# Products of messages and of the last channels on quarters of TensorE's array, in a graph network layer

## The chip, the core and the metric

The kernel runs on one core of a Trainium2 chip. The metric is the time of one execution on the device, in microseconds (us). Before the change it is 905.8 us, the median of three runs (902.68 to 907.19).

## What is computed

50,000 nodes with 160 channels (64 scalars and 32 vectors of three components), and 50,000 edges sorted by their target. For each edge a small network makes 192 weights of 16 features; the source node's channels are mixed, multiplied by these weights and by four numbers of the edge, and averaged over the edges of each target. A second mixing, a gate, and a product of the node's own channels follow, and a normalisation of each row.

```python
h = jax.nn.silu(edge_scalars @ (Wfc1 / jnp.sqrt(jnp.float32(FC_IN))))
w = h @ (Wfc2 / jnp.sqrt(jnp.float32(FC_H)))
...
f0 = x0 @ Wl1_0 * a * inv8
f1 = jnp.einsum('num,uv->nvm', x1, Wl1_1) * a[..., None] * inv32
e0 = f0[edge_src]
e1 = f1[edge_src]
...
mid0 = w0 * e0 * sh0
mid1 = w3 * jnp.einsum('eum,em->eu', e1, sh1) / jnp.sqrt(3.0)
mid2 = w1[:, :, None] * e0[:, :, None] * sh1[:, None, :]
mid3 = w2[:, :, None] * e1 * sh0[:, :, None]
...
alpha = scal @ Wa * a * inv96
out_s = scal @ Wl2_s * a * inv96
out_v = jnp.einsum('num,uv->nvm', vec, Wl2_v) * a[..., None] * inv96
conv = jnp.concatenate([out_s, out_v.reshape(n, 3 * MUL1)], axis=1)
return sc + alpha * conv
...
x = _layernorm(x + _L0_gnn_ref(x, node_vec1, ...), axis=-1)
```

Here `scal` and `vec` are the averages of mid0, mid1 and of mid2, mid3 over the edges of a node, and `sc` is the node's own channels times Wsc0 and Wsc1.

## The kernel before

The program has two stages, each written as steps that every engine runs through in its own order; semaphores alone tie the engines together.

**Edge stage.** A tile is 128 edges, a pair two tiles (t = 0, 1), a quad two pairs (k = 0, 1). A step d (98 quads, and three steps to run out) works on several quads at once:

- GpSimd gathers the source rows of quad d with four indirect DMAs (L620) into a ring of four quads.
- VectorE prepares quad d + 2 (`prepare`: sha, qprod, and its reduction; L996, L1005, L1011).
- TensorE makes the first layer (`first_layer`, L706) and the transposes of the gathered rows (`turn`, L712, L714) of quad d; ScalarE takes them out of PSUM (`take_turned`: L873, and L875 as te).
- TensorE makes, of quad d - 1, the products with source features (L732 on quarters of the array, L738 on halves) and the edge weights (L751, on halves) in `weigh`. ScalarE copies the former (L898, two copies of 512 columns).
- VectorE multiplies both into mid, for quad d - 2 (`multiply`, L1021).
- TensorE makes the products of messages of quad d - 3 (`combine`, L769 and L772): mid is the stationary operand, all 128 rows of it, and the weights wy are the moving one, 97 and 161 columns for each tile. ScalarE takes 65 of the columns into z (L883); VectorE makes the other 96 of z (L1039) and adds the message (L1045), 160 channels and a gate, in a row of 163 numbers with a count and a label that are set apart (L1029). SyncE stores the rows in DRAM.

All products are in float32, and each of these stands in the trace as two records; a transpose is one. The results of `combine` for k = 0 lie in the banks that hold the products with source features (2 and 3), those for k = 1 in banks 6 and 7; both kinds are a part of a wait:

```python
if k == 0:
    pe.wait_ge(e_out[t], min(q + 2, NS))
```

TensorE's order in a step is first layer, transposes and combine for k = 0, the same for k = 1, and `weigh`.

**Node stage.** A group is four tiles of 128 nodes (98 groups). SyncE loads windows of message rows; VectorE compares labels with columns; TensorE sums the messages of each node with the resulting 0/1 matrices (L831, 162 columns), transposes the scaled rows of the group (L817), and multiplies them with the self weights: the first 128 channels of the four tiles on quarters (L847), the last 32 channels of all four in one product over the full array (L849). ScalarE scales the sums (L943) and normalises (L921), VectorE adds the self products to x (L1391) and takes statistics (L1292), GpSimd scales the rows (L661, L664), adds (L686) and normalises a quarter (L675).

## Time and profile before

| | before |
|---|---|
| runs, us | 902.68, 905.8, 907.19 |
| profiled execution: time, span, us | 905.83, 903.9 |
| edge stage | to about 553 us of the span |
| node stage | from there to the end |
| granted clock of TensorE, mean | 0.992 |
| DMA, mean over the span | 207 GB/s |

The profile is of one execution. Its rows give, for an instruction or a group of them, the start and the time it took; an engine's instructions overlap at their ends, so the distance of two starts is often less than the first one's duration. In the chain, a piece is the time between what released an instruction and what it released.

### The profile page before, as it was taken

To read this page: it belongs to the slowest core of one execution; us is meant where nothing else is said; L and a number is where in the kernel's file an instruction comes from. 1 tells how busy PE (TensorE), PEld (TensorE's weight loads), DVE (VectorE), ACT (ScalarE), POOL (GpSimd) and SP (SyncE) were. 2 spreads that over 40 slices of the span, in tenths; PEclk is the share of its full clock that TensorE was granted. 3 is DMA by queue.
4 is the path that set the end of the run, shared out by engine and by line. 5 is a ranking of instruction groups with operands and counts; after the bars stand their busy time and mean duration, and the time that the engine had idled before them with its cause. 6 is when DMAs were issued, how large, how long until landed. Compare 5 with 4: busy or idle time off the path is not lost.

```text
span 903.9 us, 32652 instructions
## 1 busy us (share of the span) xinstructions
PE 855.1 (95%) x10688; PEld 726.4 (80%) x10688; DVE 810.6 (90%) x2797; ACT 630.4 (70%) x1961; POOL 715.3 (79%) x804
## 2 busy tenths in 40 slices
PE   2999999999998999999999988999999999999994
PEld 1788787788887877888888877888888888888884
DVE  3788999999996999999999987999999999999997
ACT  1555555555554655565565554999999999999997
POOL 6777777777776776777777712999999999999994
PEclk9999999999998999999999999999999999999998
DMA  6455544455456666567764413899999999999973
GB/s 183 121 166 165 167 137 130 133 131 143 131 135 129 187 204 190 164 172 203 208 181 132 134 64 120 249 308 314 315 318 326 310 315 312 321 304 318 319 258 146
DMA packets 87539, 186.77 MB, mean 207 GB/s; under 512 B 17646, under 2 KB 48138, under 8 KB 87371
## 3 DMA queue, kind: packets, MB, share of 16 engines
q1 hardware_dynamic: 50715, 93.00, 32.0%
q0 software_dynamic: 18944, 35.81, 18.1%
q10 hardware_dynamic: 17712, 55.87, 17.9%
q8 instruction: 87, 1.43, 0.7%
q14 instruction: 81, 0.66, 0.2%
HBM read 119.66 MB, written 64.95 MB: 204 GB/s over the span
## 4 chain that ended last, share of the span: by engine, by line
PE 70%; DVE 12%; issue 9%; POOL 5%; DMA 3%; ACT 1%; DVEq 0%; ACTq 0%; POOLq 0%
PE ps L831 20%; PE ps L772 7%; PE ps L847 7%; PE ps L751 6%; PE ps L817 6%; POOL gat L620 5%; PE ps L849 5%; PE ps L769 4%; PE ps L732 4%; PE ps L738 4%; DVE mid L1021 3%; DMA gat<-spread,srcs 3%; PE ps L714 3%; DVE z L1039 3%; PE ps L712 2%
## 5 line engine op out<-in xcount | busy, mean ns | idle before, releaser
L620 POOL DMA_INDIRECT gat<-turned,srcs x196 | 190.6, 973 | 68.9 <-issue 61.7
L620 POOL DMA_INDIRECT gat<-spread,srcs x196 | 189.5, 967 | 61.8 <-issue 59.1
L898 ACT ACTIVATE te<-ps 128x512 f32<-128x512 f32 x196 | 106.4, 594 | 124.8 <-PE ps L738 124.8
L831 PE MATMUL ps<-win,eas 60*128 60x162 f32 x2352 | 189.0, 306 | 0.7 <-DVE eas L1364 0.7
L772 PE MATMUL ps<-wy,mid 128*128 128x161 f32 x784 | 182.4, 314 | 0.0
L831 PEld LDWEIGHTS ps<-win,eas 60*128 60x128 f32 x2352 | 164.9, 186 | 17.0 <-issue 10.5
L686 POOL TENSOR_TENSOR gat<-eas,gat 128x640 f32<-128x640 f32 x98 | 152.4, 1555 | 15.2 <-ACT eas L943 12.3
L1045 DVE SCALAR_TENSOR_TENSOR msg<-ps,sha,z 128x161 f32<-128x161 f32 x392 | 151.0, 385 | 13.9
L769 PE MATMUL ps<-wy,mid 128*128 128x97 f32 x784 | 141.6, 262 | 0.2 <-DVE mid L1021 0.2
L1021 DVE TENSOR_TENSOR mid<-ps,te 128x512 f32<-128x512 f32 x196 | 133.1, 680 | 3.2 <-PE ps L751 3.2
L921 ACT ACTIVATE te<-gat,shift,rstd 128x160 f32<-128x160 f32 x292 | 131.2, 527 | 1.4 <-DVE shift L1311 1.3
L943 ACT ACTIVATE eas<-ps,coef 128x160 f32<-128x160 f32 x392 | 122.9, 402 | 9.4 <-DVE coef L1404 1.5
L769 PEld LDWEIGHTS ps<-wy,mid 128*128 128x128 f32 x784 | 123.5, 191 | 1.3 <-issue 0.7
L883 ACT ACTIVATE z<-ps 128x65 f32<-128x65 f32 x392 | 89.7, 229 | 46.1 <-PE ps L772 45.5
L772 PEld LDWEIGHTS ps<-wy,mid 128*128 128x128 f32 x784 | 119.2, 192 | 0.0
L873 ACT ACTIVATE h_sb<-ps 128x128 f32<-128x128 f32 x196 | 54.4, 278 | 75.4 <-PE ps L714 65.8
L1039 DVE TENSOR_TENSOR z<-ps,sha 128x96 f32<-128x96 f32 x392 | 97.7, 249 | 9.5 <-ACT z L883 2.8
L751 PE MATMUL ps<-h_sb,wt 64*128 64x256 f32 x784 | 102.8, 381 | 0.0
L875 ACT ACTIVATE te<-ps 128x384 f32<-128x384 f32 x196 | 94.9, 484 | 0.0
L1364 DVE TENSOR_TENSOR eas<-columns,ps 128x768 f32<-128x768 f32 x98 | 92.2, 941 | 0.1
L1292 DVE BATCH_NORM_STATS2 stats<-gat 128x6 f32<-128x320 f32 x196 | 87.1, 486 | 0.0
L664 POOL TENSOR_TENSOR eas<-xin 128x512 f32<-128x512 f32 x82 | 86.4, 1054 | 0.0
(108 smaller groups left out, 1515.1 us busy)
## 6 DMA issues: line engine op xcount, KB each, us to landing
win<-rows SPq DMA_DIRECT2D x392, 114.6 KB, 4.1
rows<-msg SPq DMA_DIRECT2D x98, 326.0 KB
out<-te ACTq DMA_DIRECT2D x47, 640.0 KB, 6.2
xin<-x_g ACTq DMA_DIRECT2D x76, 322.0 KB, 5.1
kept_x<-x_g SPq DMA_DIRECT2D x16, 322.0 KB
gat<-turned,srcs POOLq DMA_INDIRECT x196
gat<-spread,srcs POOLq DMA_INDIRECT x196
eas<-ea_t SPq DMA_DIRECT2D x7, 384.0 KB, 4.7
```

The source lines that it names most:

```text
L620: pool.indirect_dma_start(out=gat[:, slot, first:first + of.shape[1]], out_offset=None, in_=of, in_offset=bass.IndirectOffsetOnAxis(ap=src ...
L686: nc.gpsimd.tensor_tensor(res[:, slot], agg[:, b3], pre[:, b3], ALU.add).then_inc(res_ready, 1)
L751: last = nc.tensor.matmul(w_ps[:, t, 2 * c * P:2 * (c + 1) * P], wt[half, w:w + P], h_sb[half, b].rearrange("p k e -> p (k e)"), start=Tru ...
L769: nc.tensor.matmul(y[:, t, 0:W_Y1 - W_YA], mid[:, q % 2, t, 0, k, :], wy[:, 0:W_Y1 - W_YA], start=True, stop=True)
L772: nc.tensor.matmul(y[:, t, W_Y1 - W_YA:YW], mid[:, q % 2, t, 1, k, :], wy[:, of:of + VEC + 1 + MUL0], start=True, stop=True).then_inc(y_re ...
L831: last = nc.tensor.matmul(agg_ps[b1][:, 2 * h + k, 0:SW], hot[side(h), b1, k, c, :], win[side(h), (RING * i + b - 1) % WIN_RING, k, c, 0:S ...
L898: nc.scalar.activation(e_sb[:, t, :], e_ps[:, t], ACT.Copy).then_inc(e_out[t], 1)
L921: last = nc.scalar.activation(fin[:, past, k, :], res[:, past, k, :], ACT.Identity, bias=shift[:, past, k:k + 1], scale=rstd[:, past, k:k ...
L943: last = nc.scalar.activation(agg[:, b0, k, :], agg_ps[b0][:, k, 1:1 + D], ACT.Copy, scale=coef[:, b0, k:k + 1])
L1021: nc.vector.tensor_tensor(mid[:, q % 2, t].rearrange("p c k e -> p (c k e)"), w_ps[:, t], e_sb[:, t], ALU.mult).then_inc(mid_ready[t], 1)
L1039: nc.vector.tensor_tensor(z[:, k, t, 1 + MUL0:].rearrange("p (m v) -> p m v", m=3), y[:, t, 0:MUL1].unsqueeze(1).broadcast_to([P, 3, MUL1] ...
L1045: nc.vector.scalar_tensor_tensor(out=msg[:, q % 2 * QUAD + n, 0:1 + D], in0=y[:, t, Y_A:Y_C], scalar=sha[:, ring, n, 0:1], in1=z[:, k, t, ...
```

## The change

The products of messages are cut so that each uses a quarter of the array: 64 rows of mid and 64 of the 128 edges, with the moving columns in chunks of 33 (32 channels and one number more: the count, the label, the gate). A pair has 16 such products, of 32, 66 or 99 columns, in place of four. Rows of the first half of mid write into the first of the pair's two banks, rows of the second half into the second, and the lanes of both meet at the banks' border. A message row has 165 numbers. One operation of ScalarE takes z's copied chunks of both tiles, VectorE makes the other chunks in two operations for both tiles, and one operation a tile adds the message, now with count and label. The semaphores of the two tiles become one. The order of the step changes on TensorE, ScalarE and VectorE. In the node stage, the product of the last 32 channels becomes four on quarters, and the self products lie in another order, for which the host's arrays are laid out.

```diff
+CHUNK = MUL1 + 1
+CHUNKS = 5
+AW = CHUNKS * CHUNK
+SW = AW - 1
+
+
+M_A, M_C, M_S, M_B = 0, CHUNK, 2 * CHUNK, 4 * CHUNK
+CNT, LABEL, GATE = M_A + MUL1, M_C + MUL1, M_S + MUL1
...
+        def y_at(k, t, j, count=1, every=1):
+
+            flat = ps[:, (2, 6)[k]:(2, 6)[k] + 2, :].rearrange("p c e -> p (c e)")
+            lanes = flat[:, 512 - YB:512 + YB].rearrange("p (j t w) -> p j t w", t=2, w=CHUNK)
+            return lanes[:, j + 4:j + 4 + (count - 1) * every + 1:every, t, :]
...
             def combine(q, k):
-                p, y = 2 * q + k, y_ps[k]
+                p = 2 * q + k
                 if p == 1:
                     pe.wait_ge(heads_out, 2)
+                if p == 0:
+                    pe.wait_ge(wy_ready, 12)
                 for t in range(2):
-                    if p == 0:
-                        pe.wait_ge(wy_ready, 12)
                     pe.wait_ge(mid_ready[t], q + 1)
                     if k == 0:
                         pe.wait_ge(e_out[t], min(q + 2, NS))
                     if q >= 1:
                         pe.wait_ge(msg_ready[t], p - 1)
-                    nc.tensor.matmul(y[:, t, 0:W_Y1 - W_YA], mid[:, q % 2, t, 0, k, :],
-                                     wy[:, 0:W_Y1 - W_YA], start=True, stop=True)
-                    of = (W_Y1, W_Y1B)[t] - W_YA
-                    nc.tensor.matmul(y[:, t, W_Y1 - W_YA:YW], mid[:, q % 2, t, 1, k, :],
-                                     wy[:, of:of + VEC + 1 + MUL0],
-                                     start=True, stop=True).then_inc(y_ready[t], 1)
+
+
+                low, high = slice(0, HALF), slice(HALF, P)
+                made = ((0, 0, low, W_V, y_at(k, 0, -4)[:, :, 0:MUL1]),
+                        (0, 0, high, W_YA, y_at(k, 0, 1, 2)),
+                        (0, 1, low, W_Y1, y_at(k, 0, -3, 3)),
+                        (0, 1, high, W_Y1, y_at(k, 0, 0, 2, 3)),
+                        (1, 0, low, W_YA, y_at(k, 1, -2, 2)),
+                        (1, 0, high, W_V, y_at(k, 1, 3)[:, :, 0:MUL1]),
+                        (1, 1, low, W_Y1B, y_at(k, 1, -4, 2)),
+                        (1, 1, high, W_Y1B, y_at(k, 1, 0, 3)))
+                for t, c, half, w, y in made:
+                    width = y.shape[1] * y.shape[2]
+                    for edges in (low, high):
+                        last = nc.tensor.matmul(
+                            y[edges], mid[half, q % 2, t, c, k, edges],
+                            wy[half, w - W_YA:w - W_YA + width].rearrange(
+                                "p (j w) -> p j w", j=y.shape[1]), start=True, stop=True)
+                last.then_inc(y_ready, 1)
 
             def step(d):
-                if alive(d, 0):
-                    first_layer(d)
                 for k in range(2):
                     if alive(d, 0):
                         turn(d, k)
+                for k in range(2):
                     if alive(d, 3):
                         combine(d - 3, k)
                 if alive(d, 1):
-                    weigh(d - 1)
+                    find_w(d - 1)
+                if alive(d, 0):
+                    first_layer(d)
+                if alive(d, 1):
+                    find_e(d - 1)
...
-                        for sc, h in ((sca_ps, 0), (scb_ps, 1)):
+                        for h in range(2):
                             half = slice(h * HALF, (h + 1) * HALF)
                             w = W_SA - W_YA + h * HALF
                             for n in range(2):
 
                                 nodes = slice(n * HALF, (n + 1) * HALF)
-                                nc.tensor.matmul(sc[nodes, k, 0:HALF], xt[half, b1, k, nodes],
+                                nc.tensor.matmul(sc_ps[nodes, k, h], xt[half, b1, k, nodes],
                                                  wy[half, w:w + HALF], start=True, stop=True)
-                    last = nc.tensor.matmul(scb_ps[:, :, HALF:VEC], xt[:, b1, GROUP, :],
-                                            wy[:, W_SB - W_YA:W_Y1B - W_YA].rearrange(
-                                                "p (k w) -> p k w", k=GROUP),
-                                            start=True, stop=True)
+                    for h in range(2):
+                        half = slice(h * HALF, (h + 1) * HALF)
+                        w = W_SB - W_YA + h * HALF
+                        for n in range(2):
+                            nodes = slice(n * HALF, (n + 1) * HALF)
+                            last = nc.tensor.matmul(scl_ps[nodes, h], xt[half, b1, GROUP, nodes],
+                                                    wy[half, w:w + HALF], start=True, stop=True)
                     last.then_inc(sc_ready, 1)
...
             def take_second(q, k):
                 p = 2 * q + k
-                for t in range(2):
-                    act.wait_ge(y_ready[t], p + 1)
-                    if p >= 2:
+                act.wait_ge(y_ready, p + 1)
+                if p >= 2:
+                    for t in range(2):
                         act.wait_ge(msg_ready[t], p - 1)
-                    nc.scalar.activation(z[:, k, t, 0:1 + MUL0], y_ps[k][:, t, Y_C:YW],
-                                         ACT.Copy).then_inc(zc_ready[t], 1)
+                flat = ps[:, (2, 6)[k]:(2, 6)[k] + 2, :].rearrange("p c e -> p (c e)")
+                first, other = 512 - 3 * LANES, 512 + LANES + CHUNK
+                c = flat[:, first:first + 2 * (other - first)].rearrange(
+                    "p (t w) -> p t w", t=2)[:, :, 0:2 * LANES].rearrange(
+                    "p t (j w) -> p t j w", j=2)[:, :, :, 0:CHUNK]
+                nc.scalar.activation(
+                    z[:, k, :, M_S:M_B].rearrange("p t (j w) -> p t j w", j=2), c,
+                    ACT.Copy).then_inc(zc_ready, 1)
 
             def step(d):
                 for k in range(2):
                     if alive(d, 0):
                         take_turned(d, k)
+                for k in range(2):
                     if alive(d, 3):
                         take_second(d - 3, k)
+                if alive(d, 0):
+                    take_first(d)
                 if alive(d, 1):
                     q = d - 1
...
+            def finish(q, k):
+                p, ring = 2 * q + k, q % SHA_RING
+                pair = slice(2 * k, 2 * k + 2)
+                flat = ps[:, (2, 6)[k]:(2, 6)[k] + 2, :].rearrange("p c e -> p (c e)")
+                first, other = 512 - 4 * LANES, 512 + 3 * LANES + CHUNK
+                v = flat[:, first:first + other - first + MUL1]
+                dve.wait_ge(zc_ready, p + 1)
+                if p >= 2:
+                    for t in range(2):
+                        dve.wait_ge(msg_ready[t], p - 1)
+                spread = sha[:, ring, pair, :].rearrange("p t m -> p (t m)")
+                nc.vector.tensor_tensor(
+                    z[:, k, :, M_A:M_S].rearrange("p t (j w) -> p t j w", j=2)[:, :, :, 0:MUL1],
+                    two_of(v, other - first, MUL1).unsqueeze(2).broadcast_to([P, 2, 2, MUL1]),
+                    two_of(spread[:, 1:], 5, 2).unsqueeze(3).broadcast_to([P, 2, 2, MUL1]),
+                    ALU.mult).then_inc(zb_ready, 1)
+                nc.vector.tensor_tensor(
+                    z[:, k, :, M_B:M_B + MUL1],
+                    two_of(v, other - first, MUL1),
+                    two_of(spread[:, 3:], 2, 1).broadcast_to([P, 2, MUL1]),
+                    ALU.mult).then_inc(zb_ready, 1)
+                if k == 0 and q >= 2:
                     dve.wait_ge(messages_out[q % 2], 16 * (q // 2))
-                nc.vector.tensor_copy(msg[:, half, LABEL], dsts[:, QUAD * q:QUAD * (q + 1)]
-                                      ).then_inc(label_ready, 1)
-
-            def finish(q, k):
-                p, ring, y = 2 * q + k, q % SHA_RING, y_ps[k]
+                dve.wait_ge(label_ready, q + 1)
+                dve.wait_ge(zb_ready, 2 * p + 2)
                 for t in range(2):
                     n = 2 * k + t
-                    dve.wait_ge(zc_ready[t], p + 1)
-                    if p >= 2:
-                        dve.wait_ge(msg_ready[t], p - 1)
-                    nc.vector.tensor_tensor(
-                        z[:, k, t, 1 + MUL0:].rearrange("p (m v) -> p m v", m=3),
-                        y[:, t, 0:MUL1].unsqueeze(1).broadcast_to([P, 3, MUL1]),
-                        sha[:, ring, n, 1:4].unsqueeze(2).broadcast_to([P, 3, MUL1]),
-                        ALU.mult).then_inc(zb_ready[t], 1)
-                    dve.wait_ge(zb_ready[t], p + 1)
+                    y = y_at(k, t, (-1, -4)[t], CHUNKS)
                     nc.vector.scalar_tensor_tensor(
-                        out=msg[:, q % 2 * QUAD + n, 0:1 + D], in0=y[:, t, Y_A:Y_C],
-                        scalar=sha[:, ring, n, 0:1], in1=z[:, k, t, :],
+                        out=msg[:, q % 2 * QUAD + n, :].rearrange("p (j w) -> p j w", w=CHUNK),
+                        in0=y, scalar=sha[:, ring, n, 0:1],
+                        in1=z[:, k, t, :].rearrange("p (j w) -> p j w", w=CHUNK),
                         op0=ALU.mult, op1=ALU.add).then_inc(msg_ready[t], 1)
 
             def step(d):
                 if alive(d, 2):
-                    multiply(d - 2, 0)
+                    for t in range(2):
+                        multiply(d - 2, t)
                 if alive(d, 3):
                     label(d - 3)
-                    finish(d - 3, 0)
-                if alive(d, 2):
-                    multiply(d - 2, 1)
-                if alive(d, 3):
-                    finish(d - 3, 1)
+                    for k in range(2):
+                        finish(d - 3, k)
                 if alive(d, -AHEAD):
                     prepare(d + AHEAD)
```

TensorE in an edge step before, from `weigh` of one quad on (mid: the stationary operand of messages; te: turned rows and copied source products; wt, wy: weights):

```order
L732 MATMUL ps<-te,wt 64x256 x4
L738 MATMUL ps<-te,wt 128x256 x2
L751 MATMUL ps<-h_sb,wt 128x256 x4
L706 MATMUL ps<-eas,wt 128x128 x2
L712 MATMUL ps<-ident,gat 128x128
L714 MATMUL ps<-ident,gat 128x128 x2
L769 MATMUL ps<-wy,mid 128x97
L772 MATMUL ps<-wy,mid 128x161
L769 MATMUL ps<-wy,mid 128x97
L772 MATMUL ps<-wy,mid 128x161
L712 MATMUL ps<-ident,gat 128x128
L714 MATMUL ps<-ident,gat 128x128 x2
```

The same engine and place in the changed kernel, with the semaphores that an instruction waits for (L748 is the old L751, L722 the first layer, L765 and L773 the source products on halves and on quarters, L731 and L733 the transposes, L805 the products of messages):

```order
L748 MATMUL ps<-h_sb,wt 128x256 [waits mid_ready1,mid_ready0,h_out]
L748 MATMUL ps<-h_sb,wt 128x256 x3
L722 MATMUL ps<-eas,wt 128x128 [waits t_out]
L722 MATMUL ps<-eas,wt 128x128
L765 MATMUL ps<-te,wt 128x256 [waits msg_ready1,e_out0,e_out1,msg_ready0,t_out]
L765 MATMUL ps<-te,wt 128x256
L773 MATMUL ps<-te,wt 64x256 x4
L731 MATMUL ps<-ident,gat 128x128 [waits h_out,q_ready]
L733 MATMUL ps<-ident,gat 128x128 x2
L731 MATMUL ps<-ident,gat 128x128 [waits h_out,q_ready]
L733 MATMUL ps<-ident,gat 128x128 x2
L805 MATMUL ps<-wy,mid 64x32 [waits mid_ready1,e_out1,msg_ready0,msg_ready1,e_out0,mid_ready0]
```

The source products moved from ahead of L751 to the end of the step, behind the first layer, and both pairs' products now stand behind all transposes; the first of them waits for six semaphores, e_out0 and e_out1 (ScalarE's two copies) among them.

VectorE in an edge step before, from the first multiplication on:

```order
L1021 TENSOR_TENSOR mid<-ps,te 128x512
L1029 COPY msg<-dsts 128x4
L1039 TENSOR_TENSOR z<-ps,sha 128x96
L1045 SCALAR_TENSOR_TENSOR msg<-ps,sha,z 128x161
L1039 TENSOR_TENSOR z<-ps,sha 128x96
L1045 SCALAR_TENSOR_TENSOR msg<-ps,sha,z 128x161
L1021 TENSOR_TENSOR mid<-ps,te 128x512
L1039 TENSOR_TENSOR z<-ps,sha 128x96
L1045 SCALAR_TENSOR_TENSOR msg<-ps,sha,z 128x161
```

And in the changed kernel:

```order
L1080 TENSOR_TENSOR mid<-ps,te 128x512 x2
L1088 COPY z<-dsts 128x4
L1104 TENSOR_TENSOR z<-ps,sha 128x2x2x32
L1109 TENSOR_TENSOR z<-ps,sha 128x2x32
L1121 SCALAR_TENSOR_TENSOR msg<-ps,sha,z 128x165 x2
L1104 TENSOR_TENSOR z<-ps,sha 128x2x2x32
L1109 TENSOR_TENSOR z<-ps,sha 128x2x32
L1121 SCALAR_TENSOR_TENSOR msg<-ps,sha,z 128x165 x2
```

Both multiplications now stand ahead of the messages, and two operations on z are followed by two messages.

## Rows read from the trace of the kernel before

**Rows 1.** The page: busy time of each engine, share of the span, instructions.
```profile
PE 855.1 (95%) x10688; PEld 726.4 (80%) x10688; DVE 810.6 (90%) x2797; ACT 630.4 (70%) x1961; POOL 715.3 (79%) x804
```

**Rows 2.** Windows of both stages: start:end, us, busy by engine, clock, DMA share, GB/s.
```profile
420.00:520.00 100.00, 99.01 (x883) 82.74 (x880) 92.00 (x269) 58.94 (x191) 74.58 (x78) 1.00 0.60 170
700.00:800.00 100.00, 100.00 (x1829) 88.07 (x1828) 94.38 (x407) 95.90 (x294) 98.11 (x117) 1.00 0.97 313
```

**Rows 3.** Chain through one edge step: start, us, what.
```profile
306.35 0.04 issue
306.39 0.66 PE ps L732 x8
307.05 0.63 PE ps L738 x4
307.69 0.86 PE ps L751 x8
308.55 0.22 PE ps L706 x4
308.77 0.26 PE ps L712
309.03 0.22 PE ps L714 x2
309.25 0.20 PE ps L769 x2
309.45 0.30 PE ps L772 x2
...
310.24 0.11 PE ps L712
...
311.57 0.04 issue
```

**Rows 4.** Chain through one group of the node stage.
```profile
743.72 0.62 PE ps L847 x32
744.35 0.42 PE ps L849 x2
744.77 0.55 PE ps L817 x5
745.31 1.86 PE ps L831 x24
```

**Rows 5.** Timeline of GpSimd in the edge stage: start, us, instruction, idle before it.
```profile
105.26 0.95 POOL L620 DMA_INDIRECT gat<-turned,srcs  x1 [0.31 <-issue]
106.51 0.95 POOL L620 DMA_INDIRECT gat<-spread,srcs  x1 [0.30 <-issue]
```

**Rows 6.** Timeline of VectorE in an edge step.
```profile
307.82 0.17 DVE L996 TENSOR_TENSOR sha<-shs,gat 128x16 f32<-128x16 f32 x1
...
309.20 0.68 DVE L1021 TENSOR_TENSOR mid<-ps,te 128x512 f32<-128x512 f32 x1
309.80 0.16 DVE L1029 COPY msg<-dsts 128x4 f32<-128x4 f32 x1
310.10 0.26 DVE L1039 TENSOR_TENSOR z<-ps,sha 128x96 f32<-128x96 f32 x1
310.39 0.39 DVE L1045 SCALAR_TENSOR_TENSOR msg<-ps,sha,z 128x161 f32<-128x161 f32 x1
310.69 0.25 DVE L1039 TENSOR_TENSOR z<-ps,sha 128x96 f32<-128x96 f32 x1
310.97 0.38 DVE L1045 SCALAR_TENSOR_TENSOR msg<-ps,sha,z 128x161 f32<-128x161 f32 x1
```

**Rows 7.** Timeline of ScalarE in an edge step.
```profile
307.73 1.09 ACT L898 ACTIVATE te<-ps 128x512 f32<-128x512 f32 x2 [1.12 <-PE ps L738]
...
309.46 0.48 ACT L875 ACTIVATE te<-ps 128x384 f32<-128x384 f32 x1
309.83 0.23 ACT L883 ACTIVATE z<-ps 128x65 f32<-128x65 f32 x1
```

More of the change, by code:

```diff
@@ L305, in gnn_kernel @@
         mid_ready = [sem(f"mid_ready{t}") for t in range(2)]
[L306 to L308 removed]
+        y_ready = sem("y_ready")
+        zc_ready = sem("zc_ready")
+        zb_ready = sem("zb_ready")
         label_ready = sem("label_ready")
@@ L364, in edge_steps, with two_of @@
                     between[d]()
+        def two_of(flat, apart, width):
+            lanes = flat[:, 0:apart + width]
+            return bass.AP(tensor=lanes.tensor, offset=lanes.offset,
+                           ap=[lanes.ap[0], [apart, 2], [1, width]])
         def alive(d, behind):
@@ L1430, in pack_weights @@
         rows = slice(s * FC_H, (s + 1) * FC_H)
-        w[rows, W_W:W_W + P] = Wfc2[:, 0:P]
+        for c in range(2):
+            made = W_W + (c + 1 - s) % 2 * MUL0
+            w[rows, made:made + MUL0] = Wfc2[:, c * MUL0:(c + 1) * MUL0]
         col = W_W + P
@@ L1509 @@
         "dst_rows": rows(dst, EP + P, NP - 1),
-        "sh_t": tiles(rows(sh, EP)),
+        "sh_t": sh_t.reshape(P, -1),
         "ea_t": np.ascontiguousarray(
```

205 lines of the change are left out of this document (115 added, 90 removed).

## The prediction

> **What bounds the kernel now.** I read the page first, then the stretches, then the chain of each stage, and then the timeline of the engines beside TensorE. On the page TensorE is busy for 95% of the span [rows 1], but that is an average over two stages, so the stretches come next [rows 2]. In the edge stage TensorE is busy for 99.0 of 100 us, VectorE for 92.0, GpSimd for 74.6. In the node stage TensorE is busy all the time, and GpSimd (98.1), ScalarE (95.9) and the DMA engines (0.97) are nearly full as well. The clock is granted in full in both.
>
> The chain through one edge step (four tiles of edges, 98 steps) is TensorE's work almost alone [rows 3]: from 306.35 to 311.57 us, 5.22 us, of which 0.04 is issue. The reader is to see three things there. The products of messages, L769 and L772, take 0.20 + 0.30 us a tile, 2.0 us a step. A piece that follows another shape of product pays an entry: L738 has the same columns on the same halves as half of L751, whose eight records take 0.86, so it should take 0.43, and takes 0.63; the first transpose L712 takes 0.26 after products on halves and 0.11 after full ones. And L732, on quarters, takes 0.66 for eight records of 256 columns. In the node stage the period is 0.62 + 0.42 + 0.55 + 1.86 = 3.45 us a group [rows 4], again TensorE without a gap.
>
> So shorter products pay, until something else sets the period. Three candidates stand close behind. GpSimd starts a gather every 1.25 us where nothing holds it (105.26, then 106.51) [rows 5], and a step has four: **5.0 us** a step, whatever TensorE does. VectorE's instructions follow each other almost without gap [rows 6]. And ScalarE's two copies of the products with source features, L898, take 1.09 us together [rows 7]; today they lie beside L751, L706 and the transposes.
>
> **The change, part by part.** *Quarters.* From L751, 256 columns cost 0.86 / 4 = 0.215 us a record, 0.84 ns a column. A pair of tiles now has 16 products, each in two records, on four quarters: columns of 32, 66, 99 and 66 (then 66, 32, 66, 99), so 263 columns for each quarter and record. Fully even quarters give 2 x 263 x 0.84 ns = 0.44 us. If the four quarters go in rounds and a round lasts as long as its widest product (66, 99, 66, 99 = 330 columns), it is 0.55 us; the narrow ones may wait on weights besides, 0.60 us. L847 speaks for rounds of four at close to the column rate: 32 records of 64 columns are eight rounds, 8 x 64 x 0.84 = 0.43, and it takes 0.62 [rows 4], so some 0.19 is entry and nearly nothing is paid for each record. L732 says the same: two rounds of 256 are 0.43, and 0.23 is over [rows 3]. I take 0.55 a pair, 1.1 a step in place of 2.0. It is the row's shape with unequal widths, which no row shows, hence the bounds 0.44 and 0.60.
>
> *Order.* The transposes of a step now come together, then both pairs, then L751's products, the first layer, and the products with source features last, halves before quarters. The step has one entry more. TensorE alone would need: transposes 0.26 + 5 x 0.11 = 0.81; pairs 0.2 + 1.1; L751's 0.2 + 0.86; first layer 0.22; halves 0.43; quarters 0.66. That is 4.5 us.
>
> *The wait that this adds.* The pairs write into the banks from which ScalarE copies the products with source features, and these now end the step. Before the first pair stand only the transposes, 0.81 us, while the copies need 0.05 (from L738's end at 307.68 to L898's start at 307.73) + 1.09. The first product of a pair waits for both copies, since its lanes span both banks; queued behind it are everything else of the step, L751's products among it, for which VectorE waits. A wait for several semaphores costs a hand-over: the message of 310.97 ends at 311.35 [rows 6], the L732 that waits for it starts at 311.61, 0.26 later. So there is a loop: hop 0.05, copies 1.09, hand-over 0.26, entry 0.2, pairs 1.1, entry and L751's 1.06, first layer 0.22, halves 0.43, quarters 0.66 = **5.07 us**. With pairs of 0.44 it is 4.85, with 0.60 and a hand-over 0.1 longer 5.27.
>
> *VectorE.* Messages grow from 161 to 165 elements, and the eight operations of a step on z and messages stay eight. But today each message waits for the z just ahead of it (z to message 0.29, message to z 0.30 us); afterwards one wait serves two messages. From mid (0.68 long for 512 elements, 0.60 to the next start) and z (0.25 long for 96) an element costs about 1 ns, and an instruction frees the engine 0.08 before its end; so a z of 128 elements holds the engine 0.20, the one of 64 with the wait 0.25, and two messages 0.31 each: 1.07 a pair, 2.14 a step against 2.34. With two mids 1.2, a label 0.09 and the preparation 307.82 to 309.20, 1.38, it is **4.8 us**, below the other two. ScalarE makes two z copies of 132 elements in place of four of 65: at (0.48 - 0.23) / 319 = 0.8 ns an element 0.28 us each [rows 7]; less work, and not on the path.
>
> The step then follows the longest of 5.07, 5.0 and 4.8. I take 5.07: 98 x 0.15 = **15 us** less.
>
> *Node stage.* The product of the last channels, L849 (0.42), becomes four quarter products, two rounds of 64 columns: 0.11. The entry into the full array moves to the first transpose, 0.15 as in the edge stage. The sums over windows, L831, get 164 columns in place of 162: +0.02. TensorE's group would fall by 0.14 to 3.31 us. But GpSimd's 98.1% of 3.45 is 3.38, and the DMA share of 0.97 is 3.35, with rows of 165 numbers for 163 moving about 0.5% more of a group's bytes. So 3.40, of which 98 x 0.05 = **5 us** come back; 0 if the DMA engines are already the limit, 8 at 3.37. ScalarE's copies and VectorE's additions have the same number of elements as before, cut otherwise: nothing.
>
> One more small constant is set at the start; the shortest row, 0.16 us for a copy of four numbers [rows 6], says how little that is even if nothing covers it. Profiled, the kernel took 905.83 us, with 1.9 outside the span; the median of the runs is 905.8, so no correction: 905.8 - 15 - 5 = **886 us**.
>
> **The rivals.** *Floors reached.* The four quarters run almost evenly, the loop is under 5.0, gathers set the step and the group is 3.37: 98 x 0.22 + 8 = 30 us, 876. For it: L847's small cost per record. Against it: unequal widths, and the waits named.
>
> *The wait takes it all.* Pairs at 0.60 and a long hand-over make the loop 5.27, the step stays at 5.22 or so, and only the node stage gives: 901, or 905.8 if the DMA engines hold that too. For it: the copies lose nearly all of what covers them, which is what the change does to them. Against it: each of its terms must lie at its upper end.
>
> *Slower: quarters that don't overlap four deep.* If unequal products go only two at a time, a pair takes 2 x 2 x 263 x 0.84 = 0.88 us, the loop 5.73, and the time is 905.8 + 98 x 0.51 - 5 = 951. It decides from pairs of 0.63 on, where the loop reaches 5.22. For it: no row has neighbours of unequal width. Against it: L847 and L732, which go four deep. The Trainium skill, page "TensorE: Matmul & The Clock Gate", section "Wait — 56ns, not 53.3ns?", has a rule on this side: starts of products are never closer than about 25 ns. By that a pair's 32 records would take 0.80 us, an estimate, and the loop 5.57; but L847's 32 records take 0.62 us with their entry, 19 ns each, so this trace does not bear the rule out for quarters.
>
> **How the numbers follow.** Chances: forecast 0.50 (own range 879 to 896, pairs from 0.50 to 0.58), floors reached 0.19, the wait takes it all 0.20, slower 0.11. The range goes from 873 (floors, with some of the steps stretched by other work made shorter too) to 907, leaving out the slower rival and a little of the ends. A measurement of this kernel can tell about 0.5% from no change, 4.5 us. The first two cases and a third of the third are faster by more: 0.76; the rest of the third is the same, 0.13; the last is slower, 0.11.
>
> **What would show it.** In the changed profile, the step should be 5.0 to 5.15 us; ScalarE's copies should release the pairs, as a wait of TensorE of about 0.6 us a step; pairs should take 0.5 to 0.6 each; TensorE's busy share in the edge stage should fall towards 90% and GpSimd's should rise to 76% or more. In the node stage the group should be 3.37 to 3.42 us, with GpSimd or the DMA engines waited for. Wrong would be: a pair over 0.63, a step under 4.95, VectorE waited for in the loop, or a granted clock below full in the edge stage because of the new waits.

## The result, and the profile after

The changed kernel takes 920.25 us, the kernel before 904.24 us beside it on the same chip: a ratio of 1.0181, 95% interval 1.0152 to 1.021. It is slower by 1.8%; 886 us was forecast.

The page's row of busy times answers to [rows 1], the two windows to [rows 2]:

```profile
PE 797.9 (86%) x15980; PEld 628.8 (68%) x15980; DVE 796.7 (86%) x2797; ACT 606.3 (66%) x1765; POOL 711.5 (77%) x805
```
```profile
420.00:520.00 100.00, 86.44 (x1726) 62.69 (x1725) 87.06 (x262) 53.48 (x150) 70.55 (x75) 1.00 0.60 172
700.00:800.00 100.00, 94.86 (x1962) 82.11 (x1962) 90.76 (x393) 91.97 (x281) 94.05 (x113) 1.00 0.95 301
```

The reader is to see that every engine is less busy than before in both stages, at a full clock. Nothing became the bound by having more work; engines wait for each other.

Where the time went: the first group of the node stage (the count, L1349 before, L1427 after) starts at 557.5 us before and at 569.6 after, 12.1 later; the last of the 98 starts at 891.5 and 910.2, so the groups take 6.6 us more; the rest is 12.4 us in both. Together that is the 18.7 us between the two spans (903.9 and 922.6). Of the 12.1, 9.1 are there by the last preparation of a step on VectorE (531.15 and 540.24), and 3.0 come after it. The profiled execution is the longest of the four, 924.35 us.

The chain through one edge step, start, us, what, answers to [rows 3]:

```profile
444.58 1.26 PE ps L805 x44
445.83 1.08 PE ps L748 x8
446.91 0.22 PE ps L722 x4
447.13 0.07 issue
447.20 0.70 PE ps L765 x4
447.90 0.64 PE ps L773 x8
448.54 0.02 issue
...
449.06 0.60 ACT te L954
449.66 0.24 issue
449.90 1.10 PE ps L805 x39
```

It runs from the pairs' products (L805) at 444.58 to the next ones at 449.90: 5.32 us, 5.38 on average (starts of the preparation L1055, 16 steps between 425 and 510 us), where 5.07 was forecast and 5.22 was the step before. Two places differ from the forecast. L805 waits for the copies (L954), as foreseen. But the source products on halves, L765, take 0.70 in place of 0.43, after a gap of 0.07. What they wait for stands on VectorE's timeline, which answers to [rows 6]:

```profile
443.94 1.27 DVE L1080 TENSOR_TENSOR mid<-ps,te 128x512 f32<-128x512 f32 x2
...
445.70 0.29 DVE L1104 TENSOR_TENSOR z<-ps,sha 128x128 f32<-128x128 f32 x1 [0.39 <-issue]
445.91 0.21 DVE L1109 TENSOR_TENSOR z<-ps,sha 128x64 f32<-128x64 f32 x1
446.26 0.69 DVE L1121 SCALAR_TENSOR_TENSOR msg<-ps,sha,z 128x165 f32<-128x165 f32 x2
```

The two messages of pair k = 0 end at 446.95, and L765 starts 0.25 later, at 447.20. 0.25 is the hand-over that [rows 6] also show. The wait stands in the code: pair k = 0's results lie in the banks into which the source products write, so `find_e` waits for these messages, as `weigh` did before. So there is a second loop, longer than the one forecast: source products 0.70 + 0.64, copies and hand-over 1.36 (448.54 to 449.90), pair products to messages to source products 2.62 (444.58 to 447.20). The sum is 5.32, the step seen.

In the node stage most groups take 3.31 to 3.34 us, but 17 of them take more than 3.7. The waits from 600 to 880 us (engine, line, waited for: us, times, longest) name a late window:

```profile
ACT eas L999 <- DVE coef L1487: 11.5, 14, 2.1
...
DVE ps L1434 <- DMA win<-rows: 10.2, 10, 2.0
POOL gat L704 <- ACT eas L999: 7.5, 13, 0.9
```

VectorE waits for the window's transfer, ScalarE for VectorE's coefficient, GpSimd for ScalarE: one late window holds all of them.

### The profile page after: what moved, and what is told of

Same layout as the page of the kernel before. It is cut to its first block, busy times and chain, and to the rows that moved or that the text cites. A ratio compares the mean times of both kernels' runs of the same rounds, so it can differ in the third digit from the quotient of the medians.

```text
span 922.6 us, 43244 instructions
## 1 busy us (share of the span) xinstructions
PE 797.9 (86%) x15980; PEld 628.8 (68%) x15980; DVE 796.7 (86%) x2797; ACT 606.3 (66%) x1765; POOL 711.5 (77%) x805
## 4 chain that ended last, share of the span: by engine, by line
PE 48%; SPq 20%; issue 15%; ACT 8%; DVE 4%; POOL 2%; DMA 2%; ACTq 0%; DVEq 0%; POOLq 0%
SPq L484 15%; PE ps L805 13%; PE ps L748 11%; PE ps L765 7%; PE ps L773 7%; ACT te L954 6%; SPq L474 6%; PE ps L869 5%; PE ps L722 2%; PE ps L855 2%; PE ps L885 1%; DVE mid L1080 1%; POOL gat L638 1%; DMA gat<-spread,srcs 1%; DMA win<-rows 1%
## 5 line engine op out<-in xcount | busy, mean ns | idle before, releaser
L869 PE MATMUL ps<-win,eas 60*128 60x164 f32 x2352 | 193.9, 310 | 3.3 <-issue 2.7
L805 PE MATMUL ps<-wy,mid 64*64 64x66 f32 (+2 forms) x6272 | 126.6, 228 | 68.2 <-ACT te L954 56.4
L805 PEld LDWEIGHTS ps<-wy,mid 64*64 64x64 f32 x6272 | 113.4, 134 | 89.5 <-issue 84.7
L954 ACT ACTIVATE te<-ps 128x512 f32<-128x512 f32 x196 | 106.4, 595 | 94.4 <-PE ps L773 94.4
L1121 DVE SCALAR_TENSOR_TENSOR msg<-ps,sha,z 128x165 f32<-128x165 f32 x392 | 134.4, 384 | 23.2
L1080 DVE TENSOR_TENSOR mid<-ps,te 128x512 f32<-128x512 f32 x196 | 125.1, 680 | 6.4 <-issue 3.6
L748 PE MATMUL ps<-h_sb,wt 64*128 64x256 f32 x784 | 113.0, 407 | 4.0 <-DVE mid L1080 3.3
L921 ACT ACTIVATE h_sb<-ps 128x128 f32<-128x128 f32 x196 | 43.7, 274 | 97.8 <-PE ps L722 89.2
L935 ACT ACTIVATE z<-ps 128x132 f32<-128x132 f32 x196 | 55.4, 283 | 70.4 <-PE ps L805 69.9
L748 PEld LDWEIGHTS ps<-h_sb,wt 64*128 64x128 f32 x784 | 69.8, 188 | 17.5 <-issue 6.1
L1104 DVE TENSOR_TENSOR z<-ps,sha 128x128 f32<-128x128 f32 x196 | 56.0, 286 | 27.0 <-ACT z L935 23.3
L855 PE MATMUL ps<-ident,eas 128*128 128x128 f32 x490 | 74.2, 282 | 4.2 <-POOL eas L682 2.1
```

What stands on the lines that cost most here:

```text
L748: last = nc.tensor.matmul(w_ps[:, t, 2 * c * P:2 * (c + 1) * P], wt[half, w:w + P], h_sb[half, b].rearrange("p k e -> p (k e)"), start=Tru ...
L805: last = nc.tensor.matmul(y[edges], mid[half, q % 2, t, c, k, edges], wy[half, w - W_YA:w - W_YA + width].rearrange("p (j w) -> p j w", j= ...
L855: last = nc.tensor.transpose(xt_ps[:, k, :], xa[:, b % 2, k, :], ident[:])
L869: last = nc.tensor.matmul(agg_ps[b1][:, 2 * h + k, 0:SW], hot[side(h), b1, k, c, :], win[side(h), (RING * i + b - 1) % WIN_RING, k, c, 0:S ...
L954: nc.scalar.activation(e_sb[:, t, :], e_ps[:, t], ACT.Copy).then_inc(e_out[t], 1)
L1080: nc.vector.tensor_tensor(mid[:, q % 2, t].rearrange("p c k e -> p (c k e)"), w_ps[:, t], e_sb[:, t], ALU.mult).then_inc(mid_ready[t], 1)
```

## The experiments

Theory A is the loop through the messages just told. Rival B is that TensorE's own sequence and its waits for the copies make the step, and 0.70 is only how products on halves run there. For the node stage the question was whether TensorE, the wider rows or the DMA engines set the pace. Each verdict's time is beside the kernel before on the same chip; a step is the mean of the steps between 425 and 510 us.

### The copies (half_copies)

```diff
-nc.scalar.activation(e_sb[:, t, :], e_ps[:, t], ACT.Copy
+wide = 4 * P if q == 0 else 2 * P
+nc.scalar.activation(e_sb[:, t, 0:wide], e_ps[:, t, 0:wide], ACT.Copy
...
```

> The changed kernel with ScalarE copying only 256 of the 512 columns of each product with source features (from the second quad on, the other half keeps old numbers). Theory loop (source products, their copies, the first pair, its messages, source products again): each copy is 0.27 us shorter, the step falls from 5.36 by 0.4 to 0.5 and ends at the gathers' 5.0 us, about 30 us less. Rival, VectorE's string of work sets the step: it stays at 5.3 to 5.4 us.

Measured: 899.6 us, ratio 0.9946 (0.9914 to 0.9978), step 5.01. The step falls as expected, the time by 21 us and not by 30. So the copies are a link of the loop. It doesn't tell A from B, since both loops hold them.

### The second layer (w_half)

```diff
-for c in range(2):
+for c in range(2 if q < 2 else 1):
     w = W_W + c * P
```

> The changed kernel without the second half of the second layer's products (L748, its second pass over c) from the third step on; those weights keep an old value, which is the part of the computation left out. Theory A (a loop through pair k = 0's messages: source products .70 and .64, copies to the end of the second .45 and .60, hand-over .24, pair products until the z copy .81, that copy .32, z products and messages to the end of the second 1.25, hand-over .25, and round again): the second layer isn't in this loop, so the step stays at 5.40 us and the time at 916 to 924. Rival B (TensorE's own sequence: the same products and copies, then both pairs 1.26, second layer 1.08, first layer .22): the step loses .54, down to the gathers' 5.0 at best, and the time is 876 to 884.

Measured: 919.36 us, ratio 1.014 (1.0111 to 1.0168), step 5.34. TensorE has 0.54 us a step less to do, and the step gives 0.04. The chain of this kernel now goes through the messages by itself:

```profile
444.22 0.78 PE ps L805 x23
445.02 0.29 ACT z L935
445.34 0.29 DVE z L1104
446.20 0.39 DVE msg L1121
446.84 0.70 PE ps L765 x4
447.54 0.64 PE ps L773 x8
...
448.69 0.60 ACT te L954
449.54 0.78 PE ps L805 x23
```

Pair products, the z copy, z, messages, source products, copies, and the next pair products 5.32 later. TensorE's other work isn't in it. B falls, and so does the forecast's own loop as the bound: it holds L748, and 5.07 less 0.54 is 4.53.

### The messages (short_messages)

```diff
+if k or q < 2:
     nc.vector.tensor_tensor(z[:, k, :, M_B:M_B + MUL1],
...
+m = 1 if t > k and q >= 2 else CHUNKS
-y = y_at(k, t, (-1, -4)[t], CHUNKS)
+y = y_at(k, t, (-1, -4)[t], m)
```

> The changed kernel with less work on VectorE for pair k = 0 from the third step on: the second z product (L1109) is left out and the second message is made for one of its five chunks of 33 columns, so that the messages of pair k = 0 end some .4 us earlier; those columns keep old values, which is the part of the computation left out. Theory A (loop through pair k = 0's messages): the step loses .35 to .4, to the gathers' 5.0 to 5.05, and the source products on halves go back from .70 to about .45; 878 to 888. Rival B (TensorE's own sequence): the step stays at 5.35 to 5.45, 915 to 924.

Measured: 906.25 us, ratio 1.0009 (0.9979 to 1.0038), step 5.16. VectorE's shorter messages alone give 0.22 us a step and 14 us in all: A's loop is what the changed kernel lost to. (Some of the 14 lies in steps that VectorE itself fills; the part on the number of steps below tells of them.) But A expected 0.35 to 0.4 and 878 to 888 us, and the rest did not come. The chain shows why:

```profile
443.19 1.08 PE ps L748 x8
444.27 0.22 PE ps L722 x4
444.49 0.56 PE ps L765 x4
445.05 0.64 PE ps L773 x8
...
446.20 0.60 ACT te L954
446.80 0.33 issue
447.12 1.26 PE ps L805 x44
```

Here L765 starts as L722 ends: no message is waited for, and the forecast's own loop through the copies is what is left, at 443.19 + 5.19 = 448.38 for the next L748. It is 5.16 on average and not 5.07, because L765 takes 0.56 and not 0.43 and the hand-over after the copies 0.33 here and not 0.26.

### The order (old_order)

```diff
 def step(d):
+    first_layer(d)
     for k in range(2):
         turn(d, k)
-    for k in range(2):
         combine(d - 3, k)
-    find_w(d - 1)
-    first_layer(d)
     find_e(d - 1)
+    find_w(d - 1)
```

ScalarE and VectorE have the order of before as well, and quarters come ahead of halves.

> The changed kernel's products, chunks, copies and messages in the order that the kernel before had on TensorE, ScalarE and VectorE (first layer, turn and pair products k = 0, turn and pair products k = 1, source products with quarters first, second layer). Theory A (loop through pair k = 0's messages): source products 1.29, then the copies 1.29 to the hand-over or the 1.56 of second layer, first layer and first turn, whichever ends last, then 2.37 from the pair products' start to the end of the messages and .25: 5.47 a step, within .1 of the new order, 915 to 930; the order as such costs or gains little. Rival B (TensorE's own sequence, 1.29 + 1.08 + .22 + .52 + 1.26 = 4.4 without a wait): the step falls to the gathers' 5.0, 880 to 888. Rival C (the new order is what costs, the quarters cost nothing): 5.0 to 5.1 too, with the messages' wait gone.

Measured: 919.22 us, ratio 1.0129 (1.0097 to 1.0161), step 5.43. Quarters in the old order are as slow as in the new one, so rival C falls too. The chain again ends with a message that the source products (here L770) wait for:

```profile
444.19 0.72 PE ps L807 x24
444.96 0.39 DVE msg L1112
445.59 0.66 PE ps L770 x8
```

TensorE is done with the pairs at 444.91 and stands until 445.59, 0.68 us of a step.

### The loop opened (moved_results, moved_before)

TensorE's order is first layer, both turns, source products, both pairs, second layer. In moved_results ScalarE again takes the first layer beside the transposes, as in the kernel before. Banks and order go together: the waits that each needs are a part of both.

```diff
-flat = ps[:, (2, 6)[k]:(2, 6)[k] + 2, :]
+flat = ps[:, (0, 6)[k]:(0, 6)[k] + 2, :]
...
 def first_layer(q):
...
+    if q >= 4:
+        for t in range(2):
+            pe.wait_ge(msg_ready[t], 2 * (q - 4) + 1)
...
 def find_e(q):
...
-        if q >= 2:
-            pe.wait_ge(msg_ready[t], 2 * (q - 2) + 1)
...
 def combine(q, k):
...
-        if k == 0:
-            pe.wait_ge(e_out[t], min(q + 2, NS))
+    if k == 0:
+        pe.wait_ge(h_out, min(2 * q + 8, 2 * NS))
+        pe.wait_ge(t_out, min(2 * q + 8, 2 * NS))
```

> The changed kernel with the products of pair k = 0 written to the two PSUM banks of the transposes instead of those of the source products, and TensorE's order first layer, turns, source products, pair products, second layer. The source products then no longer wait for messages, nor the pair products for the copies; in exchange the first layer waits for pair k = 0's messages of the step before and pair k = 0 for the copies of the transposes. Theory A: the new loop is first layer .22, turns .52, source products 1.1 to 1.3, pair products to the end of the messages 2.37, hand-over .25 = 4.5 to 4.7, so the gathers' 5.0 set the step, and the stage's last steps, which have no gathers, run under 5: 5.0 to 5.05 a step, some 36 us less than the changed kernel, 880 to 888, with the node stage as it is. Rival: the wait moved, not gone: where the first layer waits past 5.0 for the messages, the step stands at 5.2 to 5.4, 900 to 920.

Measured: **893.5 us, ratio 0.9862 (0.9838 to 0.9886)**, the quickest version here, faster than both kernels. The step is 4.99, and VectorE's chain is now without a gap:

```profile
447.00 1.27 DVE mid L1078 x2
448.36 0.25 DVE z L1102
...
449.18 0.38 DVE msg L1119
...
450.86 0.57 DVE qprod L1062
...
451.97 1.28 DVE mid L1078 x2
```

From mid to mid it is 4.97 us, where the forecast had 4.8 for VectorE. GpSimd's gathers start 1.25 us apart here, the forecast's 5.0 for four. So both are full, and which of them holds the step isn't told apart. The time is some 6 us over the expectation: 4.99 holds in this stretch, but between 323 and 360 us steps take 5.35 to 5.5, as they take 5.44 in the kernel before, and eleven take 5.95 to 8.7. The part on the number of steps says why.

The same move with full-array products tells what the quarters give:

> The kernel before, its full-array products and messages, with only the results of pair k = 0 moved to the transposes' banks, TensorE's order of moved_results, and both products of the layers ahead of the messages on VectorE: what the loop is worth without the quarters. Theory: the loop through the messages is open here too, so TensorE's own sum decides: first layer .22, turns .52, source products 1.29, pair products 2.0, second layer .86 to 1.06 = 4.9 to 5.1 and .1 for waits: 5.0 to 5.2 a step instead of 5.22, under the changed kernel's 5.4, and a time of 885 to 903. Rival (the loop was no bound of the kernel before): 5.2 to 5.3 a step and 902 to 912.

Measured: 922.52 us, ratio 1.0221 (1.0191 to 1.0251), step 5.50. Both numbers of the expectation were wrong. TensorE is now busy for all of the window:

```profile
420.00:520.00 100.00, 100.00 (x839) 76.96 (x839) 87.55 (x256) 56.48 (x184) 68.88 (x73) 1.00 0.58 166
```
```profile
453.31 1.06 PE ps L755 x8
454.37 0.22 PE ps L709 x4
454.59 0.26 PE ps L715
...
455.40 0.59 PE ps L733 x8
455.99 0.63 PE ps L739 x4
456.63 0.39 PE ps L774 x2
```

From L755 at 453.31 to the next at 458.81 it is 5.50 us of TensorE's work: second layer 1.06, first layer 0.22, transposes 0.81 (454.59 to 455.40), source products 1.22, pair products 2.18 (456.63 to 458.81). I had put these at 4.9 to 5.1. The largest miss is the transposes, put at 0.52, which take 0.81; then there was no entry for L774 (0.39 in place of 0.20), and L755 stood at its lower end. So without quarters the moved results and their order cost time, because TensorE's own work in this order is 5.50 us; and quarters cost time without the move. Together they give 11 us, of which the node stage has a part: with its last product on the full array (moved_full_last, below) it is 6 us, 0.6%.

### The node stage

The row width alone, in the kernel before:

```diff
-AW = 3 + D
+AW = 5 + D
```

> The kernel before with two unused numbers more in each message row (165 in place of 163), nothing else. If the wider rows are what slows the node stage of the changed kernel (theory: row width), its mean group rises from 3.44 to about 3.5 us, groups of 4 us and more appear, and the time is 5 to 7 us longer. If the DMA engines are only met because the group got shorter (rival: pace), the group stays at 3.45 us, since TensorE still sets it, and the time is the same within 0.3%.

Measured: 906.01 us, ratio 0.9996 (0.9974 to 1.0017). Wider rows cost nothing there. The quarters of the last product alone, in the kernel before (node_quarters: the lines of the change on `sc_ps` and `scl_ps`):

> The kernel before with the product of the last channels on quarters alone; rows of 163 numbers, edge stage untouched. Pace: undisturbed groups are 3.3 us, but some of 4 us and more appear, and the mean is 3.4 to 3.5 us, so nothing or up to 4 us is gained and a few us may be lost. Row width: with narrow rows the mean is 3.33 to 3.36 us, and the time is about 9 us shorter.

Measured: 902.45 us, ratio 0.9967 (0.994 to 0.9994), 3 us. Their reverse (after_full_last), and the same on top of the moved results (moved_full_last):

```diff
-for h in range(2):
-    for n in range(2):
-        nc.tensor.matmul(scl_ps[nodes, h], xt[half, b1, GROUP, nodes], ...
+nc.tensor.matmul(scl_ps, xt[:, b1, GROUP, :], wy[:, W_SB - W_YA:W_Y1B - W_YA], ...
```

> The changed kernel with the product of the last channels over the full array again, in rows of 165 numbers. Pace: groups at 3.45 to 3.47 us without the long ones, so the node stage is about as long as in the kernel before (334 us), and the time is some 4 us below the changed kernel's. Row width: long groups stay, mean 3.5 us or more, and the time is that of the changed kernel or worse.

> The kernel with the moved results of pair k = 0 (moved_results), but with the product of x's last channels on the full array again, as in the kernel before: what the node stage's quarters are worth where the edge stage is quick. Theory (TensorE's .11 to .13 us a group, less what the late windows take back): 3.44 to 3.49 a group instead of 3.40, so 4 to 8 us over moved_results, 897 to 902. Rival (the node stage is the DMA engines' either way): 892 to 896.

Measured: 927.24 us, ratio 1.0243 (1.0202 to 1.0285), 7 us over the changed kernel; and 898.18 us, ratio 0.9942 (0.9922 to 0.9963), 5 us over the moved results. So quarters gain 3 us in the kernel before (the interval leaves 0.5 to 5.4) and 5 us on top of the moved results. In the changed kernel the intervals with and without them overlap, and the profiles show the difference ahead of the node stage: the groups take 341.0 us with the full array and 340.6 with quarters. The theory that only the pace of transfers counts expected after_full_last under the changed kernel, and falls. Row width forecast that run rightly, long groups included; against it stand the wider rows of rows165, which cost nothing, and node_quarters, whose profiled execution (913.88 us) has 17 long groups in narrow rows. But transfers do take something back. With half of each store, in both kernels:

```diff
-act.dma_start(block_rows(out, n), fin[:, 2 * (n % 2):2 * (n % 2) + 2] ...
+act.dma_start(block_rows(out, n)[:, 0:GROUP * D], fin[:, 2 * (n % 2)] ...
```

> The changed kernel with half of each store of the node stage's results (L1018): 320 of 640 KB are written each time, the other group of the two is not, which is the part left out. The node stage moves some 1.05 MB a group, 315 GB/s at 3.33 us; so it moves .89 MB. Theory (the DMA engines set the node stage once TensorE needs only 3.31 to 3.34 a group: the groups of 3.9 to 6.3 us are those in which a window came late): no group over 3.7 us is left but the first few, the mean is 3.31 to 3.34, the stage 321 to 324 us instead of 335 to 341, the time 904 to 909. Rival (the long groups come from SyncE's issuing or from waits among ScalarE, VectorE and GpSimd): they stay, mean 3.42 to 3.5, 915 to 924.

> The kernel before with the same half stores (the other half of the results is left out). Theory (its groups of 3.44 us are TensorE's own time, and the DMA engines keep up): the group stays at 3.43 to 3.45 and the time at 902 to 907. Rival (the DMA engines set its 3.44 too): the group falls to 3.31 to 3.38 and the time by 6 to 12 us, 893 to 899.

Measured: half_out 910.29 us, ratio 1.0078 (1.0056 to 1.01), 10 us under the changed kernel and 1 over the range expected, with 323.5 us from the first to the last group as expected; before_half_out 904.31 us, ratio 1.0009 (0.9988 to 1.0031). The window of half_out, and its longest waits from 600 to 880 us:

```profile
600.00:880.00 280.00, 279.69 (x5795) 243.52 (x5796) 272.51 (x1173) 276.91 (x841) 279.70 (x337) 1.00 0.93 279
```
```profile
PEld ps L885 <- issue: 15.0, 84, 0.2
PEld ps L869 <- DVE eas L1442: 13.8, 82, 0.2
```

TensorE and GpSimd are without a gap, no window is among the longest waits, and the transfers move 279 GB/s at a DMA share of 0.93. The same window in the changed kernel, and then in the kernel before:

```profile
600.00:880.00 280.00, 268.25 (x5516) 232.77 (x5509) 256.43 (x1107) 261.74 (x797) 266.98 (x320) 1.00 0.96 307
600.00:880.00 280.00, 280.00 (x5112) 246.57 (x5111) 263.82 (x1141) 268.36 (x813) 273.59 (x325) 1.00 0.97 312
```

The kernel before moves more, 312 GB/s, and its TensorE never stands: in this execution the transfers keep up with groups of 3.44 us. The groups, by the starts of the count (first and last of 98, their distance / 97):

| kernel | first, last, us | us a group | over 3.7 us |
|---|---|---|---|
| before | 557.5, 891.5 | 3.443 | 1 |
| before_half_out | 555.4, 889.3 | 3.442 | 1 |
| rows165 | 559.5, 892.8 | 3.436 | 1 |
| moved_before (node stage of before) | 570.4, 906.9 | 3.469 | 7 |
| node_quarters | 558.8, 899.8 | 3.515 | 17 |
| changed kernel | 569.6, 910.2 | 3.512 | 17 |
| w_half (same node stage) | 571.6, 907.5 | 3.463 | 13 |
| old_order (same) | 573.3, 905.3 | 3.422 | 7 |
| moved_results (same) | 551.1, 881.3 | 3.405 | 9 |
| half_copies (same) | 553.8, 890.7 | 3.473 | 14 |
| short_messages (same) | 555.0, 887.0 | 3.423 | 9 |
| half_out | 571.3, 894.8 | 3.335 | 1 |
| after_full_last | 573.3, 914.2 | 3.515 | 9 |
| moved_full_last | 546.2, 883.1 | 3.473 | 3 |

Before, TensorE set 3.44 and half the stores change nothing. After, TensorE needs 3.335, and what comes on top is transfers: it is gone with half the stores.

## Why the prediction was wrong

**The step that failed** is "the wait that this adds": it counted one loop, through the copies, and closed it with the pairs, L751's products, first layer, halves and quarters as if TensorE could start the source products whenever it got there. They wait for pair k = 0's messages. I had that very wait in hand: the price of the hand-over, 0.26, was read from the message of 310.97 and the L732 "that waits for it" [rows 6]. I took its price and not its place. Worked out then, it would have told the rest. In the kernel before, the source products take 0.66 + 0.63, the work up to the first pair product 0.86 + 0.22 + 0.26 + 0.22 [rows 3], and from there (309.25) through z and the messages (to 311.35) and the hand-over to the next L732 (311.61) it is 2.36: in all 5.21, the whole step. By these rows the loop was as long as TensorE's own work (5.22 less 0.04 of issue), and TensorE's 99% hid it. What quarters save on pair k = 1 lies beside it. No run takes this wait alone out of the kernel before; that the wait binds is shown for the changed kernel, by w_half and short_messages.

The change made this loop longer. The copies, which lay beside L751 and the transposes (1.56 in all), are now a link of 1.36, which is 0.20 gained. The z copy starts only after all products of a pair, 0.80 after the first (444.58 to 445.38; 0.58 before, 309.25 to 309.83). It takes 0.28 for both tiles, and VectorE makes the z of both tiles before the first message, but that adds little: from the z copy's start to the end of the messages it is 1.57, and 1.52 before. In all it is 2.62 in place of 2.36. No run here makes quarters with a z copy for each tile, so whether the 0.22 could be had back is open. And the products on halves take 0.70 after the wait. That makes 5.32, and 5.38 on average.

**The terms.** Pair products: 0.55 each and an entry of 0.2 were forecast, 1.3 for both; they take 1.26. So unequal quarters go four deep, and the rival that expected slower through two-deep quarters named the wrong mechanism: the kernel is slower, but not by this. The Trainium skill, page "TensorE: Matmul & The Clock Gate", section "Wait — 56ns, not 53.3ns?", puts starts of products at 25 ns or more; 64 records in 1.26 us are 19.7 ns each with the entry, so here too the measurement speaks against it for quarters. L748: 1.06 forecast, 1.08 measured. First layer: 0.22 and 0.22. Quarters with source features: 0.66 and 0.64. Halves: 0.43 forecast, 0.56 without a wait (short_messages) and 0.70 after one; I had given the halves no entry after the first layer. Copies with hop and hand-over: 1.40 and 1.36. The forecast's loop is thus 5.16 in short_messages, 0.09 over the 5.07; the messages' loop adds 0.22 to it.

**The other bounds.** With both loops out of the way the step stands at 4.99 (moved_results). The gathers' 5.0 holds. VectorE's 4.8 was 0.17 too low: z and messages of both pairs take 2.28 there in place of 2.14. Copies release the pairs, as forecast, with 10.7 us of waits per 100. TensorE's busy share fell to 86%, below the forecast's 90, which was the first sign that it waits for more than the copies, and GpSimd's fell to 71% where 76% or more was forecast.

**The end of the edge stage** was no term. The last steps, without gathers, start their products on VectorE 4.66 us apart before (542.38 and 547.04) and still 5.41 apart after (546.85 and 552.26), because the loop doesn't need gathers to be slow. From the last preparation to the last message it is 1.8 us more than before; the other 1.2 of the 3.0 lie between the last message and the first group, and what makes them stays open.

**The number of steps** was a term too. The 0.15 was read from steps of 5.22 us and multiplied by 98. Between the preparations of the kernel before there are 97 distances: the median is 5.22, but the mean is 5.35. In 23 of them (from 116 to 186 us, at 254 and 260, and from 323 to 356 us) VectorE has up to three operations more, which make tables for the node stage and take 0.33 to 0.74 us. Its timeline in the kernel before shows one, and the step from mid to mid is 5.44, VectorE's own:

```profile
336.20 0.67 DVE L1021 TENSOR_TENSOR mid<-ps,te 128x512 f32<-128x512 f32 x1
...
341.18 0.54 DVE L1152 TENSOR_REDUCE shortest<-spans 1x1 f32<-1x389 f32 x1
341.64 0.67 DVE L1021 TENSOR_TENSOR mid<-ps,te 128x512 f32<-128x512 f32 x1
```

Less work for TensorE hardly shortens these 23. They take 124.9 us in all before, 125.1 in the changed kernel and 122.9 in moved_results; only in short_messages, where VectorE has less to do, are they 120.9. Besides the first two distances and these, four are above 5.9 us in both kernels, and 68 are left. The changed kernel's loss lies there: they take 355.6 us before and 366.1 after. So even a loop of 5.07 would have given some 10 us (68 x 0.15, an estimate) and not 15. In moved_results the 61 that are left take 4.99 on average, but eleven are above 5.9 us, 77 us in all, and so its last preparation is only 6.1 us earlier than before (525.09). The longest of them, 8.72 us, comes after GpSimd has made four other gathers at 206 us. There VectorE waits (from 206 to 220 us):

```profile
DVE sha L1053 <- DMA gat<-spread,srcs: 3.7, 1, 3.7
```

The kernel before makes the same four gathers there and has no long step after them. A step at the gathers' own pace leaves no time to make up for such a stop; that this is the reason in all eleven isn't shown.

**The node stage** was forecast at 3.31 us for TensorE and 3.40 for the stage, 5 us less, or nothing if the DMA engines are the limit. TensorE's term was right within 0.03 (3.335 in half_out), and the edit itself gives 3 and 5 us in the two settings where it stands clear of noise. Against the 3.443 of the kernel before, the profiles of the changed node stage show nothing: six of them lie between 3.405 and 3.512, on average 3.45, and the profiled execution of the changed kernel was the worst of them. What took it back are late windows. Why they come in some executions more than in others stays open, and so does why after_full_last, which TensorE alone would hold at 3.47, has nine groups over 3.7 us, and moved_before, with the node stage of before, has seven, where the kernel before has one.

**The size.** Forecast: 15 us less in the edge stage and 5 less in the node stage. Seen in the profiled execution: 12.1 more and 6.6 more.

## What to carry to other kernels

When one engine is busy for 99% of a stage, close every loop of waits through it before costing a change: a loop through other engines can be exactly as long, and the saving of work turns into a wait. Take each wait whose price you read from the trace as a link as well, and ask whether the shortened work lies on the loop that it closes. If two loops run at the same length, shortening one gives nothing while the other stands. Here the quarters without the move were 1.8% slower and the moved results alone 2.2%, each for work or waits that it added; together they were 0.6% faster than the kernel before, and 1.4% with the node stage's quarters.

And before you multiply what a step gains by the number of steps, read the distances of all of them: a stretch where they are even is not the whole stage.

## What the runs showed of the hardware that was not expected

- Four records of 256 columns on halves take 0.56 us on TensorE after the first layer with no wait (short_messages) and 0.70 after a wait (the changed kernel); eight records in a row took 0.86, and four after quarters 0.63 [rows 3].
- A DMA share below 1.00, averaged over a stage, doesn't tell whether transfers hold engines back. From 600 to 880 us the changed kernel waits for late windows at a share of 0.96 and 307 GB/s, with TensorE busy for 268 of 280 us; the kernel before has 0.97 and 312 GB/s, and TensorE is busy all the time. With half of each store the changed kernel has 0.93 and 279 GB/s, and TensorE is busy for 279.7 us.
